# The first two attribute sets summed ahead of the main loop and placed in its last two steps

## The chip, the cores and the metric

One core of a Trainium2 chip runs the kernel. The time is device microseconds of one execution, the median of three runs: 729.02 us before (729.01 to 731.43). The engines are named as in the profile: PE (TensorE), DVE (VectorE), ACT (ScalarE), POOL (GpSimd) and SP (SyncE, which issues most of the DMAs). PEld is PE's weight load.

## The reference

A graph of 6250 nodes with 128 features and 206250 edges sorted by destination. The first layer normalizes and linearly maps the nodes, batch-normalizes them, and sums neighbours weighted by degree. The second one sums the edge attributes by destination and runs a three-layer MLP.

```python
h = jnp.maximum(_layernorm(x), 0.0)
# _L0: H = batchnorm(h @ W.T + b);  dinv = rsqrt(1 + segment_sum(ones, dst))
#      out = relu(segment_sum(H[src] * dinv[src] * dinv[dst], dst) + H * dinv**2)
x = x + _L0_gnn_ref(h, W, b, gamma, beta, src, dst)
h = jnp.maximum(_layernorm(x), 0.0)
agg = jax.ops.segment_sum(edge_attr, dst, num_segments=N)
h1 = relu(concat([h, agg, u[batch]]) @ W1 + b1)
x = x + relu(h1 @ W2 + b2) @ W3 + b3
```

## The kernel before

Data-dependent sums are made as matmuls with one-hot matrices that DVE makes by comparing indices with an iota. The program has four stages, each a block of one queue for each engine, with a barrier between blocks.

**First stage** (block at L401, to 67.7 us). The destinations are turned, the degrees counted: `make_hot` (9 batches on DVE), `count` (PE), `make_low`, `make_blocks`, `weigh_blocks` (DVE), `place_degrees` (PE). Beside it the 13 chunks of x (512 nodes; the last has 106) are normalized by DVE, ACT or POOL (`BY_POOL`, `BY_ACT`, the rest DVE; those of POOL lie in `h_far`, the others in a ring of 4), turned and mapped by PE (`turn_h`, `apply_linear`), saved by ACT, and measured by DVE (`bn_part`, L589). At the end of DVE's queue stand the span of the chunks (L615 to L619), `find_scale`, the last parts, `bn_aggr` and `begin_pass`. POOL's last work is a memset of `acc[:, 1]`, where the attribute sums are gathered later and where x lies until all chunks are normalized.

**Table stage** (block at L970, 69.9 to 114.8 us). For each chunk c: PE turns the rows (`turn_rows`, L1000) into one of three banks, ACT saves a high half (L1078), DVE a low half (`save_low_part`, L1187), PE turns both back for the self term (`turn_self`), ACT saves that. Between the chunks DVE plans where each node's edges begin, POOL gathers the sources by 17 indirect DMAs (L977), DVE splits them into low part and key (`split_sources`, 5 batches), PE turns them (`turn_keys`), ACT saves them. 16 spare tiles take what didn't fit (`key_spares` on DVE, `turn_spares` on PE, `save_spares`). At the end DVE makes the first four batches of one-hots of tiles (`hot_of_tiles`) and the attribute one-hots of set 0 (`hot_of_attr`, L904). SP loads attribute set 0 and the MLP's weights.

**Main loop** (L1396, 116.6 to 660 us). 27 steps of 80 tiles (step 17 has 16). For each tile PE builds counts (L1596), ACT evicts them by fours (L1442), and in the step after they are multiplied with the table, 98 matmuls of 240 columns (L1606). DVE makes the one-hots by eights, four batches ahead. Beside this each step handles one attribute set: 3 kinds x 5 x 4 matmuls of 128x128 f32 against 32-column one-hots (`sum_attr`, L1616; 120 records for the three kinds) into `ps_sums`, at tile 24 (`SUM_AT`; 56 from step 18 on); ACT copies them to `sums_sb` (L1451), PE places them by a one-hot from POOL (`place`, L1642) at tile 40 (72 from step 18 on), and DVE adds the windows to `acc[:, 1]` at `starts` (`add`, L1517). `summed` frees the three attribute buffers in turn: SP then loads the next set into them (1.28 MB each), and DVE makes its one-hots. PE waits for all of them (`ready_to_sum`, `ready_to_place`) in the tiles just before.

**Tail** (to 728.4 us): layer norm and MLP of the 13 chunks, with x loaded again once the last sums are made.

## Time and profile before

| | us |
|---|---|
| median of 3 runs | 729.02 (729.01 to 731.43) |
| profiled execution | 730.38 |
| its span, first to last instruction | 728.4 |
| PE busy | 666.4 (91%) |
| DVE busy | 568.1 (78%) |
| ACT busy | 456.6 (63%) |
| POOL busy | 141.8 (19%) |
| mean granted clock of PE | 0.974 |

Busy shares are a mean over stages with different limits: in the main loop PE is full, in the table stage DVE is. In the rows, an idle time before an instruction stands in brackets with what ended it; merged instructions carry their count (xN).

### The profile page before, as it was taken

The page shows a single profiled execution, that of the slowest core. Times are in us where ns is not written, and L with a number is a line of the kernel's source. Part 1 is how long each engine was busy: PE and PEld are TensorE (multiplying, and loading weights), DVE is VectorE, ACT ScalarE, POOL GpSimd, SP SyncE. Part 2 cuts the span into 40 slices and gives each one's busy share as a digit, 9 for nine tenths or more (in the row PEclk, how much of TensorE's full clock was granted, in tenths as well). Part 3 has the DMA queues.
Part 4 walks back from the last instruction along what each step waited for, and adds up shares of the span by engine and source line. Part 5 has one row for each costly group of instructions (what it writes and reads, how often), then busy time and mean ns, then how long its engine had stood idle before and what let it go on. Part 6 is the DMA issues. An engine that isn't in the chain of part 4 may idle for free. (4 is left out here: it accounts for less than half of the span.)

```text
span 728.4 us, 21542 instructions
## 1 busy us (share of the span) xinstructions
PE 666.4 (91%) x9010; PEld 572.3 (79%) x9010; DVE 568.1 (78%) x1114; ACT 456.6 (63%) x811; POOL 141.8 (19%) x184
## 2 busy tenths in 40 slices
PE   3994675899999999999999999989999999998997
PEld 2763564688888888888888888979888888896554
DVE  7888996988888888888889887588888888835632
ACT  4471682767766666666676666276666776666862
POOL 8503840111111111101111111010000000003622
PEclk9997696999999999999999999999999999999999
DMA  9000611645565554444455555465445555660122
GB/s 264 8 1 23 245 35 45 231 173 207 218 219 216 216 208 174 179 172 177 178 210 216 216 216 217 155 219 206 179 175 176 199 216 216 216 173 4 40 62 76
DMA packets 64972, 119.75 MB, mean 164 GB/s; under 512 B 3170, under 2 KB 22832, under 8 KB 64900
## 3 DMA queue, kind: packets, MB, share of 16 engines
q1 hardware_dynamic: 63332, 117.82, 46.1%
q0 software_dynamic: 576, 1.12, 0.6%
q8 instruction: 34, 0.56, 0.3%
q10 hardware_dynamic: 1008, 0.07, 0.1%
q14 instruction: 22, 0.18, 0.1%
HBM read 115.81 MB, written 4.03 MB: 165 GB/s over the span
## 5 line engine op out<-in xcount | busy, mean ns | idle before, releaser
L1606 PE MATMUL ps_product<-counts_sb,table_sb 128*128 128x240 f16 (+1 forms) x2646 | 408.5, 261 | 0.0
L1442 ACT CAST counts_sb<-ps_counts 128x588 f16<-128x588 f32 x524 | 335.8, 649 | 103.1 <-PE ps_counts L1596 59.7
L1596 PE MATMUL ps_counts<-key_hot,lo_hot 128*128 128x147 bf16 x2096 | 384.6, 231 | 16.4 <-issue 7.5
L1606 PEld LDWEIGHTS ps_product<-counts_sb,table_sb 128*128 128x128 f16 x2646 | 240.2, 97 | 8.1
L1596 PEld LDWEIGHTS ps_counts<-key_hot,lo_hot 128*128 128x128 bf16 x2096 | 198.1, 98 | 61.4 <-ACT counts_sb L1442 17.9
L898 DVE TENSOR_TENSOR key_hot<-key,iota_key 128x1176 bf16<-128x1176 f16 x262 | 199.8, 763 | 0.0
L894 DVE TENSOR_TENSOR lo_hot<-src_lo,iota_key 128x1024 bf16<-128x1024 f16 x262 | 180.8, 690 | 17.9 <-PE ps_counts L1596 15.6
L1426 POOL TENSOR_SCALAR place_hot<-iota_c,slot_now 128x96 f32<-128x96 f32 x81 | 58.7, 737 | 468.5 <-PE ps_place L1642 454.4
L904 DVE TENSOR_TENSOR attr_hot<-rel,iota_w 128x640 f32<-128x640 int16 x81 | 66.6, 824 | 57.6 <-PE ps_sums L1616 57.5
L1616 PE MATMUL ps_sums<-attr,attr_hot 128*32 128x128 f32 x3240 | 95.6, 276 | 0.0
L1616 PEld LDWEIGHTS ps_sums<-attr,attr_hot 128*32 128x32 f32 x3240 | 88.2, 111 | 4.5 <-issue 4.1
L1451 ACT COPY sums_sb<-ps_sums 128x384 f32<-128x384 f32 x27 | 12.9, 478 | 89.0 <-PE ps_sums L1616 89.0
L1517 DVE TENSOR_TENSOR acc<-acc,ps_place 128x96 f32 x81 | 20.5, 253 | 20.9 <-PE ps_place L1642 12.3
L1805 DVE TENSOR_TENSOR y_ring<-ps_three,x_ring 128x512 f32<-128x512 f32 (+1 forms) x13 | 8.6, 659 | 29.4 <-PE ps_three L1915 23.2
L977 POOL DMA_INDIRECT src_raw<-src_padded,begin_int x17 | 21.6, 1271 | 5.4 <-issue 4.9
L1642 PE MATMUL ps_place<-place_hot,sums_sb 128*128 128x96 f32 x162 | 22.0, 272 | 0.0
L873 ACT ACTIVATE attr<-attr,nodes_below 128x128 f32<-128x128 f32 x49 | 20.2, 496 | 0.8 <-DVE nodes_below L864 0.8
L1783 POOL TENSOR_TENSOR x_ring<-attr,b_rows 128x512 f32<-128x512 f32 (+1 forms) x13 | 15.6, 1204 | 25.7 <-DVE y_ring L1805 25.7
L1642 PEld LDWEIGHTS ps_place<-place_hot,sums_sb 128*128 128x128 f32 x162 | 20.2, 191 | 0.0
L1852 ACT ACTIVATE z_ring<-ps_one,cols 128x512 f32<-128x512 f32 (+1 forms) x13 | 8.7, 673 | 16.0 <-PE ps_one L1904 16.0
L1893 PE MATMUL ps_two<-z_ring,w_sb 128*128 128x512 f32 (+1 forms) x26 | 13.6, 606 | 4.7 <-ACT z_ring L1859 2.5
L1078 ACT ACTIVATE table_sb<-ps_rows,dinv 128x128 f16<-128x128 f32 x49 | 14.0, 390 | 5.6 <-PE ps_rows L1000 5.6
(294 smaller groups left out, 526.7 us busy)
## 6 DMA issues: line engine op xcount, KB each, us to landing
attr<-in_edge_attr_dram SPq DMA_DIRECT2D x80, 1280.0 KB, 8.2
acc<-in_x_dram SPq DMA_DIRECT2D x4, 768.0 KB, 9.4
attr<-in_x_dram SPq DMA_DIRECT2D x12, 256.0 KB, 5.2
out_dram<-y_ring SPq DMA_DIRECT2D x12, 256.0 KB, 2.3
src_padded<-in_src_dram SPq DMA_DIRECT2D x1, 805.5 KB
attr<-in_edge_attr_dram SPq DMA_DIRECT2D x2, 320.0 KB, 8.1
attr<-in_edge_attr_dram SPq DMA_DIRECT2D x1, 640.0 KB, 3.9
raw_d<-in_dst_dram SPq DMA_DIRECT2D x1, 480.0 KB
```

Of the source, the lines that this page charges most:

```text
L873: ins = act.activation(h2_ring[:, c % 2, k * P:(k + 1) * P], x_again[:, n, :], ACT.Relu, scale=rstd[:, n:n + 1], bias=shift[:, n:n + 1])
L894: v.tensor_tensor(lo_hot[:, held], src_lo[:, tiles].rearrange("p (b c) -> p b c", c=2).unsqueeze(2).to_broadcast(whole), iota_lo[:].unsque ...
L898: v.tensor_tensor(key_hot[:, held], key[:, tiles].rearrange("p (b c) -> p b c", c=2).unsqueeze(2).to_broadcast(whole), iota_key[:].unsquee ...
L904: v.tensor_tensor(attr_hot[:, r], rel[:, r, :, s * CG:(s + 1) * CG].unsqueeze(3).to_broadcast(whole), iota_w[:].unsqueeze(1).unsqueeze(1). ...
L977: pool.indirect_dma_start(src_raw[:, k, :], None, src_elements, bass.IndirectOffsetOnAxis(ap=begin_int[:, k:k + 1], axis=0))\
L1426: pool.tensor_scalar(place_hot[:, n % R, :], iota_c[:], slot_now[:, kind, s:s + 1], None, ALU.is_equal).then_inc(place_hots, 1)
L1442: act.copy(counts_sb[s % 2][:].rearrange("p h (n t) -> p h n t", n=WN) [:, :, :, k * QUAD:(k + 1) * QUAD], ps_counts[n % 2][:, :, 0:KEYS]. ...
L1517: v.tensor_tensor(win, win, ps_place[:, kind * WC:(kind + 1) * WC], ALU.add)\
L1596: ins = pe.matmul(ps_counts[quad % 2][:, c, 0:KEYS], lo_hot[:, held, pair, :, q % 2], key_hot[:, held, pair, :, q % 2], start=True, stop=True)
L1606: ins = pe.matmul(ps_product[side][:, 0:SLOTS] if tiles == TS else product, table_sb[:, h, low, :], counts_sb[side][:, h, :] if tiles == T ...
L1616: ins = pe.matmul(ps_sums[g * W:(g + 1) * W, j * P:(j + 1) * P], attr_hot[:, j, t, g, :], attr[:, j * CG + g, t * P:(t + 1) * P], start=(t ...
L1642: pe.matmul(ps_place[:, j * WC:(j + 1) * WC], sums_sb[:, j, :], place_hot[:, j, :], start=True, stop=True).then_inc(placed, 1)
```

## The change

Attribute sets 0 and 1 are summed by PE in the table stage: set 0 behind `turn_rows(5)`, `turn_self(3)` and `plan_before` into the bank `ps_lows`, set 1 at the very end into a bank of `ps_rows`. ACT saves them (`save_early`) to `early_sums`, which lies over `drel`, no longer needed. The one-hots of set 0 are made at the end of the first stage on DVE, those of set 1 between `split_sources(3)` and `hot_of_tiles(0)`. SP issues set 1's loads as set 0's sums are made, and set 2's loads as set 1's are. The main loop sums sets 2 to 26 in steps 0 to 24, and steps 25 and 26 only place sets 0 and 1 (`set_of_place`). Step 0 sums at tile 56 and places at 72; its attribute one-hots stand between batches 4, 5, 6 and 7.

In the first stage POOL normalizes chunks 4 and 7 too, DVE's small work (scale, span, `make_low(0)`, `make_blocks(0)`) moves between the degree one-hots, and the memset of `acc[:, 1]` is cut into a piece for each chunk, each behind the chunk's normalization, and one for the end.

```diff
+        drel_flat = sb("drel", [P, R * GB * GT], I16)
+        drel = drel_flat[:].rearrange("p (g t) -> p g t", t=GT)
...
+        EARLY = 2
+        LATER = STEPS - EARLY
+        attr_hot = sb("attr_hot", [P, R, GT, CG, W])
+        early_hots, early_summed, early_saved = (sem(n, ctx) for n in ("early_hots", "early_summed", "early_saved"))
+        early_in = [sem(f"early_in{r}", ctx) for r in range(R)]
+        early_sums = drel_flat[:, 0:2 * EARLY * R * P].bitcast(F32)\
+            .rearrange("p (e j f) -> p e j f", e=EARLY, j=R)
+
+        def set_of_place(s):
+            return s + EARLY if s < LATER else s - LATER
+
+        def hot_of_attr(engine, s, r, made):
+            whole = [P, GT, CG, W]
+            engine.tensor_tensor(attr_hot[:, r], rel[:, r, :, s * CG:(s + 1) * CG].unsqueeze(3).to_broadcast(whole),
+                                 iota_w[:].unsqueeze(1).unsqueeze(1).to_broadcast(whole), ALU.is_equal)\
+                  .then_inc(made, 1)
+
+        def early_hot(engine, e):
+            for r in range(R):
+                if e >= 1:
+                    engine.wait_ge(early_summed, (e - 1) * R + r + 1)
+                hot_of_attr(engine, e, r, early_hots)
...
-            BY_POOL, BY_ACT = (5, 8, 11), (2, 3, 6, 9)
+            BY_POOL, BY_ACT = (4, 5, 7, 8, 11), (2, 3, 6, 9)
...
-                    pool.wait_ge(h_by_pool, len(BY_POOL))
-                    pool.wait_ge(h_by_dve, len(BY_DVE))
-                    pool.wait_ge(h_by_act, len(BY_ACT))
-                    pool.memset(acc[:, 1, :], 0.0)
+                    for c in range(CHUNKS):
+                        h_is_ready(pool, c)
+                        pool.memset(acc[:, 1, c * NC:c * NC + width(c) * P], 0.0)
+                    pool.memset(acc[:, 1, NB * P:], 0.0)
...
-                    normalize(4)
-                    for b in range(4, BATCHES):
-                        make_hot(v, b)
+                    make_hot(v, 4)
+                    make_hot(v, 5)
                     make_low(v, 0)
+                    make_hot(v, 6)
+                    make_hot(v, 7)
+                    v.wait_ge(w_in, 16 * W_LOADS)
+                    find_scale(v, link)
+                    find_span()
                     link(make_blocks(v, 0))
-                    normalize(7)
+                    make_hot(v, 8)
                     bn_part(0)
                     bn_part(1)
...
                     for c in range(5, 8):
                         bn_part(c)
-                    v.tensor_copy(chunk_start[:], chunk_row[:, 0, :].rearrange("a (r s) -> a s r", r=R))
-                    link(v.tensor_tensor(chunk_row[:, 1, :], chunk_row[:, 1, :], chunk_row[:, 0, :], ALU.subtract))
-                    link(v.tensor_reduce(span_row[:, 1:2], chunk_row[:, 1, :], AX.X, ALU.max))
-                    link(v.tensor_scalar(span_row[:, 0:2], span_row[:, 0:2], 0.0, None, ALU.max))
-                    v.tensor_copy(span_int[:], span_row[:, 0:2])
-
-                    v.wait_ge(w_in, 16 * W_LOADS)
-                    find_scale(v, link)
                     for c in range(8, CHUNKS):
                         ins = bn_part(c)
                     link(ins)
                     v.bn_aggr(bn[:, 0:2], bstats[:].rearrange("p c k -> p (c k)")).then_inc(bn_ok, 1)
                     begin_pass(v, link)
+                    early_hot(v, 0)
                     v.wait_ge(placed_deg, CC)
...
+        def load_early(sp):
+            for e in range(1, EARLY):
+                for r in range(R):
+                    sp.wait_ge(early_summed, (e - 1) * R + r + 1)
+                    load_attr(sp, e * R + r, CG, early_in)
+            for r in range(R):
+                sp.wait_ge(early_summed, (EARLY - 1) * R + r + 1)
+                load_attr(sp, EARLY * R + r, CG, attr_in)
+
+        def sum_set(pe, sums, j, summed_up):
+            for t in range(GT):
+                for g in range(CG):
+                    ins = pe.matmul(sums[g * W:(g + 1) * W, j * P:(j + 1) * P], attr_hot[:, j, t, g, :],
+                                    attr[:, j * CG + g, t * P:(t + 1) * P], start=(t == 0), stop=(t == GT - 1))
+            ins.then_inc(summed_up, 1)
+
+        def sum_early(pe, e, sums):
+            for j in range(R):
+                pe.wait_ge(early_hots, e * R + j + 1)
+                pe.wait_ge(early_in[j], 16 * (e + 1))
+                sum_set(pe, sums, j, early_summed)
+
+        def save_early(act, e, sums):
+            act.wait_ge(early_summed, (e + 1) * R)
+            act.copy(early_sums[:, e].rearrange("p j f -> p (j f)"), sums[:, 0:R * P]).then_inc(early_saved, 1)
...
+                        if c == 5:
+                            sum_early(pe, 0, ps_lows)
                         if c == 7:
+                            pe.wait_ge(early_saved, 1)
                             turn_keys(0)
...
                     turn_spares(pe, spare_keys_at, spare_lows_at, spares_keyed, spares_turned)
+                    pe.wait_ge(low_ready, CHUNKS)
+                    sum_early(pe, 1, ps_rows[0][:].rearrange("p b f -> p (b f)"))
...
                         if c == 6:
+                            save_early(act, 0, ps_lows)
                             save_low(0)
...
+                    save_early(act, 1, ps_rows[0][:].rearrange("p b f -> p (b f)"))
...
                     split_sources(3)
+                    early_hot(v, 1)
                     v.wait_ge(keys_saved, 1)
                     hot_of_tiles(v, 0, 0)
                     split_sources(4)
                     key_spares(v, link, spare_in, spares_keyed)
                     for b in range(1, HELD):
                         hot_of_tiles(v, b, b * OCT)
-                    for r in range(R):
-                        hot_of_attr(v, 0, r)
                     save_spares(v, spare_keys_at, spare_lows_at, spares_turned)
...
+                    load_early(sp)
...
-                            for a in range(R, CC):
+                            for a in range((EARLY + 1) * R, CC):
                                 c, r = divmod(a, R)
-                                sp.wait_ge(summed, a - R + 1)
+                                sp.wait_ge(summed, a - (EARLY + 1) * R + 1)
...
-                                sum_at, place_at = ((LATE_SUM_AT, LATE_PLACE_AT) if s > SHORT else (SUM_AT, PLACE_AT))
+                                sum_at, place_at = ((LATE_SUM_AT, LATE_PLACE_AT) if s > SHORT or s == 0 else
+                                                    (SUM_AT, PLACE_AT))
                                 for b in range(HELD if s == 0 else 0, OCTS):
                                     make_oct(s, b)
+                                    if s == 0 and b < HELD + R:
+                                        make_attr_hot(b - HELD)
                                     if s == LATE and b == 2:
                                         make_attr_hots(s)
                                     if s == LATE and b == 3:
                                         add(SHORT)
                                     if s >= 2 and s != LATE + 1 and b == 3:
                                         take_product(s - 2)
...
-                                    if s < STEPS - 1 and b == min(sum_at // OCT + 2, OCTS - 1):
+                                    if s + 1 < LATER and b == min(sum_at // OCT + 2, OCTS - 1):
                                         make_attr_hots(s + 1)
-                                    if s < SHORT and b == place_at // OCT + 3:
+                                    if 0 < s < SHORT and b == place_at // OCT + 3:
                                         add(s)
-                                    if s > LATE and b == 1:
+                                    if (s > LATE or s == 1) and b == 1:
                                         add(s - 1)
...
+                                early = like == 8
                                 for q in range(TS):
-                                    if q == sum_at - 1:
+                                    if q == sum_at - 1 and not early:
                                         pe.wait_ge(attr_hots, s * R + R)
                                     build_tile(quads, octs, q, first, OCTS * odd)
                                     if q == LAG and like >= 3:
                                         pe.wait_ge(taken, s - 2)
-                                    ready_to_sum(s, first, sum_at - q)
-                                    ready_to_place(s, first, place_at - q)
+                                    if not early:
+                                        ready_to_sum(s, first, sum_at - q)
+                                    ready_to_place(s, first, place_at - q, early)
...
-                                        sum_attr(s)
+                                    if q == sum_at and not early:
+                                        sum_attr()
                                     if q == place_at:
-                                        place(s)
+                                        place(early_sums[:, s - LATER] if early else sums_sb)
...
-                            with pe.Fori(LATE // 2 + 2, (STEPS + 1) // 2) as i:
+                            with pe.Fori(LATE // 2 + 2, (LATER + 1) // 2) as i:
                                 step(i, 1, 7)
                                 step(i, 0, 7)
+                            step((LATER + 1) // 2, 1, 8)
+                            step((LATER + 1) // 2, 0, 8)
...
```

## Rows read from the trace of the kernel before

**Rows 1.** the page: busy shares, and TensorE's granted clock in 40 slices (tenths)

```profile
PE 666.4 (91%) x9010; PEld 572.3 (79%) x9010; DVE 568.1 (78%) x1114; ACT 456.6 (63%) x811; POOL 141.8 (19%) x184
...
PEclk9997696999999999999999999999999999999999
```

**Rows 2.** timeline (start us, us, engine line operation), TensorE, two late steps

```profile
620.63 3.48 PE L1616 MATMUL ps_sums<-attr,attr_hot 128*32 128x128 f32 x120
624.05 0.24 PE L1596 MATMUL ps_counts<-key_hot,lo_hot 128*128 128x147 bf16 x1
...
640.73 3.48 PE L1616 MATMUL ps_sums<-attr,attr_hot 128*32 128x128 f32 x120
```

**Rows 3.** windows: us, busy of the engines, granted clock, DMA share, GB/s

```profile
70.00:83.00 13.00, 9.49 (x64) 8.00 (x65) 12.19 (x46) 7.17 (x24) 9.47 (x9) 0.50 0.95 337
...
84.00:90.00 6.00, 3.33 (x35) 2.54 (x35) 5.96 (x17) 2.64 (x9) 5.09 (x4) 1.00 0.14 36
94.00:110.00 16.00, 10.49 (x166) 8.98 (x163) 14.38 (x46) 14.44 (x38) 6.27 (x8) 1.00 0.11 27
110.00:116.60 6.60, 0.00 (x0) 0.00 (x0) 4.77 (x9) 0.00 (x0) 0.39 (x1) 0.57 0.00 0
116.60:123.00 6.40, 5.67 (x61) 4.19 (x65) 2.75 (x4) 3.60 (x6) 1.15 (x3) 0.50 0.02 5
124.80:135.30 10.50, 7.96 (x117) 5.40 (x105) 9.31 (x16) 8.22 (x15) 2.70 (x3) 1.00 0.99 368
```

**Rows 4.** timeline of TensorE in step 0 and at the start of step 1

```profile
116.62 1.17 PE L1596 MATMUL ps_counts<-key_hot,lo_hot 128*128 128x147 bf16 x8 [7.48 <-issue]
118.04 1.23 PE L1596 MATMUL ps_counts<-key_hot,lo_hot 128*128 128x147 bf16 x8 [0.25 <-ACT counts_sb L1442]
...
121.17 5.10 PE L1616 MATMUL ps_sums<-attr,attr_hot 128*32 128x128 f32 x120
126.19 0.66 PE L1596 MATMUL ps_counts<-key_hot,lo_hot 128*128 128x147 bf16 x7
...
131.76 1.00 PE L1596 MATMUL ps_counts<-key_hot,lo_hot 128*128 128x147 bf16 x8 [0.19 <-ACT counts_sb L1442]
...
135.98 0.26 PE L1606 MATMUL ps_product<-counts_sb,table_sb 128*128 128x240 f16 x1
...
140.03 2.17 PE L1616 MATMUL ps_sums<-attr,attr_hot 128*32 128x128 f32 x72
```

**Rows 5.** timeline of the first stage's end, POOL, DVE and ACT

```profile
57.19 5.39 POOL L503 MEMSET acc<- 128x6346 f32 x1 [24.81 <-DVE h_ring L571]
...
59.46 3.15 DVE L618 TENSOR_SCALAR span_row<-span_row 1x2 f32<-1x2 f32 x1
...
61.09 0.35 ACT L682 ACTIVATE acc<-turn,cols 128x106 f32<-128x106 f32 x1 [2.03 <-PE turn L755]
...
64.06 2.64 DVE L589 BATCH_NORM_STATS2 bstats<-acc 128x6 f32<-128x512 f32 x5
...
67.54 0.19 DVE L629 TENSOR_TENSOR dinv<-dinv,ps_x 128x49 f32<-128x49 f32 x1
```

**Rows 6.** timeline of the first stage's middle, POOL and DVE

```profile
25.64 6.74 POOL L497 TENSOR_SCALAR h_far<-acc,rstd,shift 128x128 f32<-128x128 f32 x12 [4.15 <-DVE shift L129]
...
36.34 1.35 DVE L274 TENSOR_TENSOR deg_hot<-drel,iota_deg 128x1080 bf16<-128x1080 int16 x2 [2.34 <-PE ps_y L309]
```

**Rows 7.** timeline of the table stage about chunk 6, PE and DVE

```profile
85.52 0.66 PE L1000 MATMUL ps_rows<-ident,acc 128*128 128x128 f32 x4
...
90.18 1.12 DVE L1187 SCALAR_TENSOR_TENSOR table_sb<-ps_rows,dinv,table_sb 128x128 f16<-128x128 f32 x4
```

**Rows 8.** timeline of the table stage's start and end, SP, PE and DVE

```profile
69.95 2.64 SPq L880 DMA_DIRECT2D attr<-in_edge_attr_dram  x3
...
108.93 0.21 PE L242 MATMUL ps_plan<-ident,spare_lows 16*128 16x16 f32 x1
...
112.33 2.28 DVE L904 TENSOR_TENSOR attr_hot<-rel,iota_w 128x640 f32<-128x640 int16 x3
```

More of the change, by code:

```diff
@@ L1330, in gnn_kernel, with _ @@
                     with nc.Block() as block:
+                        @block.sync
+                        def _(sp):
+                            for a in range(R):
+                                load_attr(sp, a, CG, early_in)
+                            load_early(sp)
+                        @block.scalar
+                        def _(act):
+                            for e in range(EARLY):
+                                save_early(act, e, ps_sums)
                         @block.gpsimd
@@ L1355, in _ @@
                             first_hots_of_pass(v)
+                            for e in range(EARLY):
+                                early_hot(v, e)
                 with nc.Fori(0, chunk_passes) as chunk_pass:
@@ L1636, in ready_to_place, with place @@
                                     pe.wait_ge(added, s * R)
[L1637 removed]
+                                if before == 1 and not early:
                                     pe.wait_ge(sums_saved, s + 1)
[L1640 removed]
+                            def place(sums):
                                 for j in range(R):
[L1642 removed]
+                                    pe.matmul(ps_place[:, j * WC:(j + 1) * WC], sums[:, j, :], place_hot[:, j, :],
                                               start=True, stop=True).then_inc(placed, 1)
```

80 lines of the change are left out of this document (35 added, 45 removed).

## The prediction

> **What bounds the kernel now.** I read the page first [rows 1]: TensorE (PE) is busy for 91% of the span, and its clock digits have one weak stretch, slices 4 to 7. Next comes the spacing of like events in the main loop. Two neighbouring blocks of attribute sums start at 620.63 and 640.73, so a late step takes 20.10 us, and the first build behind the block starts at 624.05 [rows 2]: a block of 120 matmul records holds PE for 3.42 us. PE has work without a pause there and sets the pace, so what leaves its queue is time.
>
> Then the windows by stage [rows 3]. From 70 to 83 the granted clock stood at 0.50, which is 1.2 of its 2.4 GHz; in 84 to 90 and 94 to 110 it was 1.00. In this table stage (69.9 to 114.8) PE is far from full and VectorE (DVE) nearly is: 14.38 of 16 us in 94 to 110. So added DVE or queue time costs there, added PE time not always. In step 0 the block of sums took 5.02 us (121.17 to 126.19) [rows 4], because the clock was still 0.50 from 116.6 to 123 [rows 3].
>
> The first stage ends on DVE. Its 1x2 tensor_scalar (L618) lasted from 59.46 to 62.61, and the memset on GpSimd (POOL) ended at 57.19 + 5.39 = 62.58; only then came the scale and the last five bn parts (64.06 to 66.70), and DVE ended at 67.73 [rows 5]. ScalarE (ACT) had saved the last linear chunk by 61.44, having waited 2.03 us for PE [rows 5]: PE sets that time.
>
> **Steps 25 and 26.** They now hold no sums; step 25 places set 0 and step 26 set 1. PE keeps 80 builds, 98 multiplies and the place. What could be late next is the eviction or DVE. But between two blocks the loop already runs 20.10 - 3.42 = 16.68 us at a stretch without sums, ACT and DVE keeping up. So this is 2 x 3.42 = **-6.8 us**. The extra unrolled PE code I cost at nothing: steps 0 to 2 and 18 to 20 are unrolled already.
>
> **Step 0.** Its sums (now set 2) move from tile 24 to 56, its place from 40 to 72. Before, tile 0 starts at 116.62 and the first product, behind the fifth tile of step 1, at 135.98 [rows 4]; less 0.6 for those builds, the step took 18.7. The block now falls after the clock has risen: 5.02 becomes 3.42, -1.6. Eight builds come every 1.42 us at the low level (116.62 to 118.04) and every 1.00 + 0.19 = 1.19 at the full one [rows 4]; two more eights now lie ahead of the rise, 2 x 0.23 = +0.4. Estimate **-1.2**, step 0 being 17.5. DVE has three attr hots between its first batches; at 2.28/3 = 0.76 each [rows 8] the batch for tile 56 is ready just in time.
>
> **Wait for set 3.** Its three loads are issued as set 2's sums end. Before, the same three transfers moved from 124.8 to 135.3 (10.5 us at 0.99 of the DMA engines) [rows 3], to 9.1 behind the end of the sums at 126.2 [rows 4]. Now the sums end near T0 + 12.9 (T0 is tile 0), so the data are there at T0 + 22.0 to 22.6. Step 1 wants them at tile 23: its block came 4.05 behind the first product (140.03), so about 4.5 behind its tile 0, T0 + 22.0. Estimate **+0.4**, bounds 0 and 1.0. Later sets have a whole step of 20 us.
>
> **First stage.** POOL normalizes two more chunks, 8 more instructions at 6.74/12 = 0.56: it ends near 36.9 instead of 32.4 [rows 6], each chunk before PE wants it. DVE loses chunks 4 and 7. It idled 2.34 us for PE's counting before hot 6 [rows 6], and once more as long before hot 8; make_low(0), scale and span (1.45 us behind L618 and some 0.7 ahead of it [rows 5]) now fill this. The memset goes in fourteen pieces, 0.43 us for 512 of 6346 columns, the last ones near 56. DVE then has bn parts 5 to 11 done and waits for 61.44. Behind it come the last part (106 columns, about 0.3 by 2.64/5 = 0.53 for a full one), then the aggregate, begin_pass and dinv, 66.70 to 67.73 = 1.03 [rows 5]. New there is early_hot(0), three attr hots: 2.28 [rows 8]. End: 61.44 + 0.1 + 0.3 + 1.03 + 2.28 = 65.1, against 67.73: **-2.6**. Bounds: -2.8, and 0 if DVE loses its slack of some 2 us before 61.
>
> The L618 row shows a DVE instruction that ended with the POOL memset beside it. The Trainium skill, "SBUF — State Buffer", section "Who interferes with whom", says that a tensor_scalar in a two-port mode and a GpSimd instruction lock each other out for the whole instruction. That speaks against the new order, since pieces of the memset now meet the scale's and span's four tensor_scalars: by it up to 4 x 0.43 = 1.7 us, which the slack holds; were it all on the path, the sum would be 1.7 less good.
>
> **Table stage, set 0.** SP issues the three loads first, as it did [rows 8]; they fill the DMA engines until about 84 (0.95 in 70 to 83, 0.14 in 84 to 90) [rows 3]. PE takes the block ahead of turn_rows(6), which started at 85.52 [rows 7]. The clock was 1.00 there, so 3.42 us: the rows of chunk 6 are turned at 89.5, and ACT, which needs about as long for them as DVE (1.12), has them at 90.8. DVE began low part 6 at 90.18 [rows 7]: 0.6 late. ACT then holds save_early, one copy, ahead of save_low(0), and PE's turn_keys(0) waits for both; DVE has other work meanwhile. Estimate +0.3, bounds 0 and +3.4 (the block at half the clock).
>
> **Table stage, set 1.** early_hot(1) costs DVE 2.28 and the old attr hots are gone: 0. But the hots stand ahead of split 4 and key_spares, so turn_spares, over at 109.1 [rows 8], now ends near 111.3. Only behind it comes the second block, with PE idle for some 2.3 us before: 114.7 at the full level, 118.1 at half of it. The clock did fall back after 109.1 (mean 0.57 in 110 to 116.6) [rows 3]. Step 0's block of 5.02 is 56 records at half rate (3.2 us) and 64 at full; I take the same mix again here, 5.0, ending 116.3 less 0.1 to 0.3 of lead: 116.1. Behind it SP must still issue the last of set 2's loads, 2.64/3 = 0.88 [rows 8], with ACT's copy beside it: 117.0. Before, DVE's hots ended at 114.61 [rows 8] and two small copies at 114.8. **+2.2**, bounds +0.7 and +4.1. Set 2 lands near 126, 9.1 behind these sums' end by the same pattern as set 3, and step 0 wants it at about 128.
>
> Set 1's own load runs from 87 to 99 beside the gathers of src. Splits 2 to 4, which need the later gathers, stand behind low part 12 in DVE's order, so I cost this at nothing; bound +1.
>
> **Sum.** -6.8 - 1.2 + 0.4 - 2.6 + 0.3 + 2.2 = **-7.7 us**. The profiled execution took 730.38 us for a span of 728.4; it would be 722.7. The median of the runs is 729.02, and 729.0 - 7.7 = **721.3**.
>
> **The rivals.** (A) *All fits.* The second block runs at the full level (+0.7), the first costs nothing, set 3 is in time: -9.9, **719.1**. For it: the clock was 1.00 through 94 to 110 with PE idle a third of that time; against it: the longer idle stretch. (B) *The early sums are paid for.* One of the two blocks runs wholly at half the clock, or DVE waits for gathers behind set 1's load: -7.7 + 3.1 = -4.6, **724.4**, and with both 726.3. For it: 13 us at 0.50 at the stage's start, and a DVE without slack; against: 1.00 from 84 on. (C) *The first stage gives nothing.* DVE comes later than 61.4 by more than it gains, or PE does: -7.7 + 2.6 = -5.1, **723.9**. For it: PE works without a pause up to there, so a late h chunk moves the end. (D) *Slower than before.* The blocking wait for set 0 sits in the middle of PE's queue, with rows, tables and keys of all later chunks behind it; each microsecond that the third load lands past 86 goes through ACT to DVE. It eats the gain of 7.7 from about 94 on; if the loads take twice their 14 us (to 98), the stage is 12 longer: **733**. Against it: the DMA engines were free from 84 to 90 (0.14) [rows 3]. (E) That the sums don't leave the loop is excluded: PE's queue of steps 25 and 26 holds none.
>
> **How the numbers follow.** Forecast 721.3 (720.0 to 722.6) 0.45; A 0.18; B 0.17; C 0.13; D 0.02; between or beyond these 0.05. The range takes in A and B's first price, with the half microsecond on either side that the small terms leave open: 718.4 to 724.9. B's upper part, D and the tails are left out. A measurement here tells about 0.5% (3.6 us): faster than 725.4 has 0.92, within it 0.06, slower 0.02.
>
> **What would show it.** In the changed profile: the first stage's last DVE instruction at about 65.1, and the span's tensor_scalar short; a block of 3.4 us near 83 (2.6 earlier than 85.5) and one of 3.4 to 6.8 at the end of the table stage; PE's first build within 0.5 of 116.6; step 0's block at 3.42; at most 1 us of PE idle before step 1's; no block in the loop's last two steps, whose places lie 16.7 us apart. The forecast is wrong if these steps take 20 us, if DVE waits in the table stage for more than 3 us in all, or if PE's clock falls inside the loop.

## The result, and the profile after

The changed kernel took **735.2 us** (median of 6 runs, 732.0 to 736.0) against 729.1 (728.7 to 731.5) for the kernel before on the same chip: ratio 1.0058, 95% interval 1.0035 to 1.0082 (taken over all runs, so it is not that of the two medians). It is slower by some 0.6%, where 721.3 with a range of 718.4 to 724.9 was forecast. Its profiled execution took 736.01 us for a span of 734.1. The executions of each kernel spread by some microseconds (see the first stage below), so most of what follows compares stretches of the profiled executions.

The stretches, each from its two end marks in the two traces:

| stretch | before | after | difference | forecast |
|---|---|---|---|---|
| start to DVE's last operation of the first stage | 67.73 | 67.00 | -0.73 | -2.6 |
| from there to the last operation of any engine in the table stage | 47.04 | 49.60 | +2.56 | +2.5 |
| from there to PE's first build in the main loop | 1.85 | 7.95 | **+6.10** | 0 |
| first build to ACT's copy of step 1's sums | 26.96 | 31.39 | **+4.43** | -0.8 |
| the steps behind it, to the copy of step 24's sums | 460.52 | 460.60 | +0.08 | 0 |
| from there to the end | 124.30 | 117.56 | -6.74 | -6.8 |
| sum | 728.4 | 734.1 | +5.7 | -7.7 |

The page of the changed kernel (busy shares, granted clock in 40 slices, and the main loop's multiplies with what ended the idle time before them), beside [rows 1]:

```profile
PE 672.2 (92%) x9010; PEld 577.4 (79%) x9010; DVE 565.3 (77%) x1106; ACT 457.3 (62%) x811; POOL 150.4 (20%) x205
...
PEclk9997686799999999999999999999999999999999
...
L1677 PE MATMUL ps_product<-counts_sb,table_sb 128*128 128x240 f16 (+1 forms) x2646 | 408.8, 261 | 2.8 <-DMA attr<-in_edge_attr_dram 2.8
```

The loop now has a stall on a load of attributes that it didn't have. The timeline shows the rest of it. The end of the table stage and the entry into the main block, PE first, then ACT, POOL and SP:

```profile
112.37 0.26 PE L240 MATMUL ps_plan<-ident,spare_lows 16*128 16x16 f32 x1
112.56 3.48 PE L921 MATMUL ps_rows<-attr,attr_hot 128*32 128x128 f32 x120
...
124.55 1.17 PE L1667 MATMUL ps_counts<-key_hot,lo_hot 128*128 128x147 bf16 x8 [8.50 <-issue]
...
116.12 0.48 ACT L933 COPY drel<-ps_rows 128x384 f32<-128x384 f32 x1 [3.44 <-PE ps_rows L921]
...
118.06 1.55 POOL L1494 TENSOR_SCALAR place_hot<-iota_c,slot_now 128x96 f32<-128x96 f32 x3 [16.05 <-issue]
...
113.93 2.55 SPq L905 DMA_DIRECT2D attr<-in_edge_attr_dram  x3
```

Set 1's block runs at the full rate (3.48 us), and the last operation of the stage ends at 116.12 + 0.48 = 116.60, with SP's last issue over at 116.48. POOL is in the main block at 118.06. PE is there 6.49 us later, waiting for nothing that the profile names ("issue"). In the kernel before, POOL's first operation of the block started at 116.21 and PE's first build at 116.62 [rows 4], 0.41 apart:

```profile
116.21 1.54 POOL L1426 TENSOR_SCALAR place_hot<-iota_c,slot_now 128x96 f32<-128x96 f32 x3 [14.11 <-issue]
```

What PE did in this time stands in the view by source line, which lists branches too. It is the jump over the block that this data never enters, `If(slot_pass > 0)`, on PE's sequencer (PEldq). The line is executed twice, at 117.7 and 668.5 after the change; its shortest, median and longest time are in ns, after and then before:

```profile
L1423 PEldq COMPARE_BRANCH  x2: 82/3192/6302, 117.7 to 668.5; - x2
```
```profile
L1356 PEldq COMPARE_BRANCH  x2: 82/158/234, 115.9 to 663.1; - x2
```

The first of the two took 6.30 us in place of 0.23. The same branch took 0.07 us at most on every other engine.

Then step 0 and the start of step 1 on PE, which answer to [rows 4], and the window of the builds (columns as in [rows 3]):

```profile
130.21 1.23 PE L1667 MATMUL ps_counts<-key_hot,lo_hot 128*128 128x147 bf16 x8 [0.19 <-ACT counts_sb L1510]
131.63 1.23 PE L1667 MATMUL ps_counts<-key_hot,lo_hot 128*128 128x147 bf16 x8 [0.19 <-ACT counts_sb L1510]
133.04 1.23 PE L1667 MATMUL ps_counts<-key_hot,lo_hot 128*128 128x147 bf16 x8 [0.18 <-ACT counts_sb L1510]
...
134.76 4.31 PE L921 MATMUL ps_sums<-attr,attr_hot 128*32 128x128 f32 x120
139.00 0.66 PE L1667 MATMUL ps_counts<-key_hot,lo_hot 128*128 128x147 bf16 x7
...
150.67 0.38 PE L1677 MATMUL ps_product<-counts_sb,table_sb 128*128 128x240 f16 x1 [2.82 <-DMA attr<-in_edge_attr_dram]
...
151.30 4.56 PE L921 MATMUL ps_sums<-attr,attr_hot 128*32 128x128 f32 x120
```
```profile
124.55:136.00 11.45, 9.99 (x81) 6.66 (x85) 10.00 (x15) 8.43 (x14) 0.00 (x0) 0.50 0.12 46
```

All eights of step 0 run at the low level, 1.42 us apart, until the block of sums starts. In step 1 PE stands still for set 3's loads, and the block behind that stall takes 4.56 us.

### The profile page after: what moved, and what is told of

It is laid out like the page before. It is cut to its first block and busy times, and to the rows that moved or that the text cites. A ratio compares the mean times of both kernels' runs of the same rounds, so it can differ in the third digit from the quotient of the medians.

```text
span 734.1 us, 21496 instructions
## 1 busy us (share of the span) xinstructions
PE 672.2 (92%) x9010; PEld 577.4 (79%) x9010; DVE 565.3 (77%) x1106; ACT 457.3 (62%) x811; POOL 150.4 (20%) x205
## 3 DMA queue, kind: packets, MB, share of 16 engines
HBM read 115.81 MB, written 4.03 MB: 163 GB/s over the span
## 5 line engine op out<-in xcount | busy, mean ns | idle before, releaser
L1667 PEld LDWEIGHTS ps_counts<-key_hot,lo_hot 128*128 128x128 bf16 x2096 | 199.2, 98 | 61.9 <-ACT counts_sb L1510 17.8
L921 PE MATMUL ps_sums<-attr,attr_hot 128*32 128x128 f32 x3000 | 89.0, 277 | 0.0
L921 PEld LDWEIGHTS ps_sums<-attr,attr_hot 128*32 128x32 f32 x3000 | 82.0, 112 | 4.4 <-issue 3.9
L1707 PE MATMUL ps_place<-place_hot,sums_sb 128*128 128x96 f32 x150 | 20.4, 272 | 0.0
L1707 PEld LDWEIGHTS ps_place<-place_hot,sums_sb 128*128 128x128 f32 x150 | 18.7, 191 | 0.0
```

Of the source, the lines that this page charges most:

```text
L921: ins = pe.matmul(sums[g * W:(g + 1) * W, j * P:(j + 1) * P], attr_hot[:, j, t, g, :], attr[:, j * CG + g, t * P:(t + 1) * P], start=(t == ...
L1667: ins = pe.matmul(ps_counts[quad % 2][:, c, 0:KEYS], lo_hot[:, held, pair, :, q % 2], key_hot[:, held, pair, :, q % 2], start=True, stop=True)
L1707: pe.matmul(ps_place[:, j * WC:(j + 1) * WC], sums[:, j, :], place_hot[:, j, :], start=True, stop=True).then_inc(placed, 1)
```

## Experiments

Eleven more kernels ran; e11 is the changed kernel once more. "Entry gap" is the time from POOL's first operation in the main block to PE's first build there; "step 0/1" is the time from that build to the copy of step 1's sums.

| kernel | code PE jumps over, added | set 2's loads meanwhile | entry gap | step 0/1 | ratio to before (95%) |
|---|---|---|---|---|---|
| before | 0 | none | 0.41 | 26.96 | 1 |
| changed | 120 matmuls | yes | 6.49 | 31.39 | 1.0058 (1.0035-1.0082) |
| e11, changed again | 120 | yes | 6.54 | 31.99 | 1.0075 (1.0046-1.0105) |
| e1 | 120 | a quarter | 3.97 | 31.86 | 1.0063 (1.0047-1.0080) |
| e2, from before | 0 | 3.8 MB, other | 0.40 | 26.98 | 0.9998 (0.9981-1.0015) |
| e3 | 120 | none | 3.63 | 34.65 | 1.0072 (1.0045-1.0099) |
| e4 | 120 | yes | 6.61 | 30.21 | 1.0120 (1.0097-1.0143) |
| e5 | 0 | yes | 0.40 | 31.47 | 0.9989 (0.9968-1.0010) |
| e6, from before | 120 | none | 4.03 | 26.89 | 1.0062 (1.0037-1.0086) |
| e7 | 120 | yes | 6.43 | 27.25 | 0.9984 (0.9956-1.0012) |
| e8 | 60 | yes | 0.62 | 32.39 | 0.9987 (0.9964-1.0009) |
| e9 | 60 | yes | 0.63 | 29.12 | 0.9937 (0.9906-0.9967) |
| e10 | 120 | yes | 6.54 | 27.79 | 0.9992 (0.9966-1.0018) |

**The gap ahead of the first build.** In the first four kernels, Theory 1 was that PE's next instructions come behind set 2's loads, and Theory 2 that the larger program of PE makes the change of block slow whatever the loads do.

e1 makes set 2's loads a quarter as large:

```
-                load_attr(sp, EARLY * R + r, CG, attr_in)
+                load_attr(sp, EARLY * R + r, 1, attr_in)
```

> The changed kernel, with set 2's three loads at the end of the table stage cut to a quarter (one group of four; the other three groups keep set 1's rows, so set 2's sums are not the reference's). Theory 1 (PE's next instructions come over the DMA engines and stand behind these loads): the traffic after the stage ends 7.5 us sooner, and the gap from the last instruction of the table stage (116.6) to PE's first build falls from 7.9 us to 2 to 4; the time falls by 4 to 6 us. Theory 2 (the longer PE program makes the block change slow, whatever the DMAs do): the gap stays at 7.9 and the time moves by less than 1 us. The wait for set 3 in step 1 stays at about 3 us in both.

Measured: 734.3 us (732.3 to 734.8), gap 3.97. The loads are worth 2.5 us of the gap, and 4 us stay (0.4 of them as in the kernel before).

e2 gives the kernel before the same traffic, from DRAM to DRAM, at the same place:

```
+                    sp.wait_ge(spares_turned, 1)
+                    for a in range(R):
+                        sp.dma_start(spill[a], edge_attr[...]...).then_inc(spilled, 16)
```

> The kernel before, with three DMAs of 1.28 MB each from DRAM to DRAM, issued by SP once PE has turned the spares (109.1), that nobody reads. Nothing else is changed. Theory 1: they keep the DMA engines busy until 10 to 20 us later, and PE's first build, now at 116.6, comes 4 to 12 us later; the time rises by as much. Theory 2: PE starts at 116.6 to 117, and the time is within 1 us of the kernel before, since no load is wanted before 122.

Measured: 729.5 (728.0 to 733.2), gap 0.40. Traffic alone does nothing: Theory 1, as it stood, is refuted.

e3 issues set 2's loads only behind PE's first build:

```
+                            sp.wait_ge(built, 1)
+                            for r in range(R):
+                                load_attr(sp, EARLY * R + r, CG, attr_in)
```

> The changed kernel, with set 2's loads moved from the end of the table stage into the main loop's queue of SP, behind PE's first quad of builds. Theory 1: the gap before the first build falls from 7.9 us to about 1.9, the sums of step 0 then wait for set 2 (landing some 12 us behind the start, wanted at 10): 2 us of it go back, so 3 to 4.5 us less in all than the changed kernel. Theory 2: the gap stays, and the wait comes on top: 2 us more than the changed kernel.

Measured: 735.3 (732.1 to 737.5), gap 3.63, and PE then waited for set 2 in step 0. So 3.2 us of the 6.1 that were added have nothing to do with the loads. Two rivals were left. Theory 3: the cost lies in code that PE jumps over. In the `If(slot_pass > 0)` block, which this data never enters, the change had put the early sums as 120 unrolled matmuls. Theory 4: PE always takes some 7 us from its last matmul of the table stage to its first build (109.14 to 116.62 before), and is now last in the stage.

e5 takes those never-executed matmuls out of the changed kernel:

```
-                            for e in range(EARLY):
-                                if e >= 1:
-                                    pe.wait_ge(early_saved, e)
-                                sum_early(pe, e, ps_sums)
```

> The changed kernel without the 120 matmuls of the early sums in the block for later slot passes, which this data never enters: every instruction that is executed stays as it was, PE's program is only shorter just ahead of the main block. Changed kernel: 735.2 us; PE's first build at 124.55, 6.5 us behind POOL's entry into the block. Theory 3 (code that PE jumps over has to be fetched past): the first build comes 0.4 to 1 us behind POOL's entry, that is at about 118.5 to 119.5, and the time is 729 to 731. Theory 4 (PE's own path from the last instruction of the table stage to the first build takes some 7 us whatever it jumps over, and it is now last in the stage): first build and time unchanged, 124 to 125 and 735.

e6 puts as many into the same block of the kernel before:

```
+                            for e in range(2):
+                                for j in range(R):
+                                    for t in range(GT):
+                                        for g in range(CG):
+                                            pe.matmul(ps_sums[...], attr_hot[:, j, t, g, :], attr[...], ...)
```

> The kernel before with 120 more matmuls in the block for later slot passes, which this data never enters: nothing that is executed is changed, PE's program is longer just ahead of the main block. Kernel before: 729.1 us; PE's first build at 116.62, 0.4 us behind POOL's entry. Theory 3 (code that PE jumps over has to be fetched past): first build some 3 us later, at 119.5 to 120, time about 732. Theory 4 (PE's own path from its last instruction of the table stage counts): PE ends that stage at 109 as before, so first build at 116.6 and time 729.

Measured: e5 729.7 (725.6 to 731.2) with a gap of 0.40, e6 734.3 (733.1 to 738.1) with a gap of 4.03. PE's and POOL's lines at the entry, of e5 and then of e6:

```profile
119.00 1.54 POOL L1490 TENSOR_SCALAR place_hot<-iota_c,slot_now 128x96 f32<-128x96 f32 x3 [17.23 <-issue]
...
112.03 4.96 PE L921 MATMUL ps_rows<-attr,attr_hot 128*32 128x128 f32 x120
119.40 0.72 PE L1663 MATMUL ps_counts<-key_hot,lo_hot 128*128 128x147 bf16 x8 [2.41 <-issue]
```
```profile
119.93 1.54 POOL L1434 TENSOR_SCALAR place_hot<-iota_c,slot_now 128x96 f32<-128x96 f32 x3 [14.45 <-issue]
...
112.66 0.21 PE L242 MATMUL ps_plan<-ident,spare_lows 16*128 16x16 f32 x1
...
123.96 1.17 PE L1604 MATMUL ps_counts<-key_hot,lo_hot 128*128 128x147 bf16 x8 [11.10 <-issue]
```

e5 executes what the changed kernel executes, and e6 what the kernel before executes. In e5 PE goes from its last sum (116.99) to its first build in 2.41 us, so Theory 4 is refuted too. Theory 3 is shown from both sides: 120 matmuls that are never run cost 3.2 (e3) to 3.6 us (e6), and 6.1 with set 2's loads in flight.

The branch itself shows it in all thirteen traces. Here it is in e6 and in e8 (60 matmuls, see below):

```profile
L1364 PEldq COMPARE_BRANCH  x2: 82/1957/3832, 119.6 to 670.3; - x2
```
```profile
L1425 PEldq COMPARE_BRANCH  x2: 82/264/447, 115.5 to 661.3; - x2
```

It takes 0.23 us in before, e2 and e5, 0.44 to 0.45 in e8 and e9, 3.44 to 3.83 in e3, e1 and e6, and 6.24 to 6.42 in the five with 120 matmuls and the full loads. The DMA records say more. In each of the eight traces with 120 matmuls, one packet of the kind "instruction" (16 KB, on queue 8) moves while the branch lasts, and the branch ends 1.31 to 1.42 us behind it. It starts 1.0 to 1.25 us into the branch in e3, e6 and e1, and 3.57 to 3.65 us into it where set 2's loads fill the queues. In the other five traces no such packet moves during the branch. So PE waits there for code to be fetched, and loads in flight put off the fetch, which is what Theory 1 had right. One link is inferred: the records don't say for which engine a packet is.

**Step 0.** e7 puts its sums back to tile 24, its place back to tile 40, and DVE's three one-hots together ahead of it (DVE's lines left out here):

```
-                                sum_at, place_at = (LATE_SUM_AT, LATE_PLACE_AT) if like >= 5 or first else (SUM_AT, PLACE_AT)
+                                sum_at, place_at = (LATE_SUM_AT, LATE_PLACE_AT) if like >= 5 else (SUM_AT, PLACE_AT)
```

> The changed kernel with step 0 put back: its sums at tile 24 and its products at tile 40, as in the kernel before, and DVE makes the three one-hots of set 2's attributes at once in step 0. From the first build to the copy of step 1's sums the changed kernel takes 31.39 us, the kernel before 26.96. Theory: the difference is the clock, which the 60 dense matmuls of the sums block at tile 24 raised and the builds alone do not, and the wait for set 3's loads, which leaves with it, as they are issued 8 us sooner. Then the stretch is 27.0 and the time 735.2 - 4.4 = 730.8. Rival (the wait moves on: set 3's loads or the one-hots made at the step's start hold PE up): the stretch stays over 29 and the time over 733.

Measured: 729.4 (725.6 to 732.4); step 0/1 took 27.25 us in place of 31.39. The sums at tile 56, meant as a gain of 1.2 us by the prediction, cost 4.1 with the wait for set 3 that comes of them.

e10 keeps tile 56 and makes set 3's loads a quarter as large; e11 is the changed kernel beside it:

```
-                                load_attr(sp, a, groups, attr_in)
+                                load_attr(sp, a, 1 if a < (EARLY + 2) * R else groups, attr_in)
```

> The changed kernel with the three loads of set 3, issued as step 0's sums end, a quarter as large; three quarters of set 3's rows keep what set 2 left there. From PE's first build to the copy of step 1's sums the changed kernel took 31.39 us, the kernel before 26.96, and PE waited 2.82 us for set 3 in it. If the wait is the larger cause: the stretch is 31.39 - 2.82 = 28.6 and the time 2.8 us below the changed kernel's; the 1.6 us that stay over the kernel before are the clock. If the wait only hides another one (the one-hots of set 3, PE's own pace), the stretch stays at 30 or more. The gap ahead of the first build stays at 6 to 8 us behind PE's last sum in both.

> The changed kernel itself, on the same chip and in the same rounds as e10_quarter_set3, for the comparison of the two and for a second look at it. Theory 3 and the load's wait: as in its first profile, PE's first build 6 us or more behind POOL's entry, 31.4 us from there to the copy of step 1's sums, and 735. If the gap ahead of the first build was an accident of the first profile, the first build comes within 1 us of POOL's entry.

Measured: e10 731.2 (727.6 to 733.0), e11 736.9 (733.2 to 738.9), before 731.1 beside them. PE at step 1 in e10, then in e11:

```profile
148.12 3.48 PE L921 MATMUL ps_sums<-attr,attr_hot 128*32 128x128 f32 x120
```
```profile
152.09 0.32 PE L1677 MATMUL ps_product<-counts_sb,table_sb 128*128 128x240 f16 x1 [2.68 <-DMA attr<-in_edge_attr_dram]
...
152.65 4.90 PE L921 MATMUL ps_sums<-attr,attr_hot 128*32 128x128 f32 x120
```

Without the wait the stretch is 27.79, against 31.99 in e11: 4.2 us less, of which 2.7 are the wait and 1.4 the block behind it (4.90 against 3.48). That leaves 0.8 us over the kernel before for step 0's low clock and late block. The expectation had put the wait at 2.8 and the clock at 1.6; the stall has its own cost in clock behind it. The medians differ by 5.8 us, the two profiled executions by 6.1; in these, 1.6 of the 1.9 us beyond this stretch lie in the first stage, which ended at 65.89 in e10 and at 67.49 in e11.

**The first stage.** e4 gives the changed kernel the old order of the first stage, with the new one-hots of set 0 kept at its end:

```
-                    make_hot(v, 4)
-                    make_hot(v, 5)
+                    normalize(4)
+                    for b in range(4, BATCHES):
+                        make_hot(v, b)
...
-                        pool.memset(acc[:, 1, c * NC:c * NC + width(c) * P], 0.0)
+                    pool.memset(acc[:, 1, :], 0.0)
```

> The changed kernel with the first stage of before (chunks 4 and 7 on DVE, one memset, span and scale at the end), early_hot(0) kept at its end. If the reordering of the first stage gained what its forecast says, this is 4.9 us slower than the changed kernel (67.7 + 2.3 against 65.1 where it should have ended). By the trace of the changed kernel, where that stage ended at 67.0, it is 3.0 us slower: 70.0 to 67.0. If the new order itself made PE late there (its matmuls ran at half rate until about 40.4 instead of 36.2), PE ends at 61.0 again here and the time is 1 us slower or less.

Measured: 737.2 (735.6 to 739.0). That is 2.0 us above the changed kernel by the medians and 0.6% by the ratios (1.0120 against 1.0058), so the times alone can't tell an expectation of 4.9 from one of 3.0; the traces can. The start of PE's last row of matmuls in the stage (two of `turn`) against DVE's end, over all traces: in the old order 60.62 and 67.73 (before), 64.02 and 71.13 (e2), 64.34 and 71.43 (e6), that is 7.1 us every time, and in e4, with the 2.28 us of one-hots more, 58.62 and 67.94, that is 9.3. In the new order, one-hots included, nine traces give 4.34 to 4.36, from 58.11 and 62.46 (e9) to 63.29 and 67.63 (e3). The gain is 2.76 us, as far as the new order doesn't move PE's own end. That end lies anywhere from 58.1 to 64.3, in either order; the means are 61.9 and 62.1, from which a shift of a microsecond can't be excluded. What moves it is PE's rate: its counting matmuls start 0.100 us apart at first and 0.055 apart from 31 us in e4, 35.8 in before, some 41 in the changed kernel and 43 in e6, and the last row then starts at 58.62, 60.62, 62.65 and 64.34. (In e1, e3, e5 and e11 the rate rises at 36 to 37, but the granted clock is 0.50 again from 53 to 57.) Both orders have early and late ones. Between before and e2, which run the same work, this is all of the difference of the spans (3.4 of 3.4 us); between the two profiles of the changed kernel it is 0.5 of 2.1.

**Both repairs.** e8 is e7 with the 120 matmuls as a loop over the two sets, 60 in the program, for all data:

```
-                            for e in range(EARLY):
-                                if e >= 1:
-                                    pe.wait_ge(early_saved, e)
-                                sum_early(pe, e, ps_sums)
+                            with pe.Fori(0, EARLY) as e:
+                                for j in range(R):
+                                    pe.wait_ge(early_hots, e * R + j + 1)
+                                    pe.wait_ge(early_in[j], e * 16 + 16)
+                                    sum_set(pe, ps_sums, j, early_summed)
+                                pe.wait_ge(early_saved, e + 1)
```

> Step 0 put back as in e7_step0_at_24, and in the block for later slot passes the early sums as a loop over the two sets, 60 matmuls of code in place of 120; it computes what the changed kernel computes on any data. e5 (no such code) had PE's first build 0.40 us behind POOL's entry and 729.7, e7 (step 0 put back, 120 matmuls) 6.4 us and 729.4. If the two causes are separate, their gains add: with 60 matmuls jumped over for free the first build is 0.4 us behind POOL's entry and the time 729.4 - 5.5 = 723.9. If any code beyond what the kernel before had costs in proportion, the gap is about 3 us and the time about 726.5. If the causes overlap (the same late start counted twice), the time stays at 728 to 729.5.

Measured: 730.2 (725.2 to 731.5), no better than e5 or e7 alone. The gap is gone (0.62), but PE is now early enough to meet set 2's loads in step 0:

```profile
122.38 0.30 PE L1668 MATMUL ps_counts<-key_hot,lo_hot 128*128 128x147 bf16 x1 [2.21 <-DMA attr<-in_edge_attr_dram]
125.62 0.30 PE L1668 MATMUL ps_counts<-key_hot,lo_hot 128*128 128x147 bf16 x1 [2.94 <-DMA attr<-in_edge_attr_dram]
125.86 5.70 PE L921 MATMUL ps_sums<-attr,attr_hot 128*32 128x128 f32 x120
```

The gap of 6.5 us had hidden these loads in e7. With it gone, a wait of 2.21 + 2.94 = 5.15 us and a block of 5.70 us, mostly at the low level, took its place.

e9 takes set 1 off the end of the table stage, so that set 2's loads start sooner:

```
                     for b in range(2, KEY_BATCHES):
                         turn_keys(b)
+                        if b == 2:
+                            pe.wait_ge(low_ready, CHUNKS)
+                            sum_early(pe, 1, ps_rows[0][:].rearrange("p b f -> p (b f)"))
...
-                    split_sources(3)
                     early_hot(v, 1)
+                    split_sources(3)
```

> e8_looped_pass_code with the sum of set 1 taken off the end of the table stage: DVE makes its one-hots ahead of the split of the fourth batch of sources, PE sums it between the third and fourth batch of keys, ScalarE copies it ahead of the last two batches of keys. In the changed kernel PE's block ran 112.5 to 116.0 with its copy to 116.6, behind DVE's last operation at 115.9. Expected: block at 107.5 to 111, set 2's loads issued by 112, PE and ScalarE done before DVE, POOL's entry at 117.2 in place of 118.0 to 119.0, and the time 1 to 2 us below e8. Rival: the block delays the keys that are behind it on PE, and with them DVE's end; then DVE ends after 117 and the time is that of e8 or more.

```profile
102.75 3.48 PE L921 MATMUL ps_rows<-attr,attr_hot 128*32 128x128 f32 x120
...
112.56 1.17 PE L1669 MATMUL ps_counts<-key_hot,lo_hot 128*128 128x147 bf16 x8 [4.61 <-issue]
...
118.27 0.31 PE L1669 MATMUL ps_counts<-key_hot,lo_hot 128*128 128x147 bf16 x1 [1.65 <-DMA attr<-in_edge_attr_dram]
```

Measured: **726.4** (721.7 to 729.5, 8 runs), ratio 0.9937 (0.9906 to 0.9967): faster than the kernel before and than the changed one. That is a gain of 0.6%, and by the medians 3.9 us below e8, where 1 to 2 were expected. Set 1's block is over at 106.2, and the wait in step 0 falls from 5.15 to 1.65 us. DVE ends the stage 45.8 us after it starts, as in e8 (45.9), so the rival, keys that come late to DVE, is refuted. From DVE's last operation of the first stage to the last of the table stage it is 48.0 us in place of 48.7. This profiled execution (721.7) is the fastest of its runs, with PE early in the first stage; the median is the fair number.

## Why the prediction was wrong, step by step

**Steps 25 and 26** (-6.8): right, -6.74. The last two places lie 16.56 us apart (636.15 and 652.71), without sums.

**"The extra unrolled PE code I cost at nothing"**: this step failed, and it is the larger error. I looked only at code that is executed in the loop, and took the 1.85 us between the stage's end and the first build as fixed. 120 matmuls in a block that is skipped make it 7.95 (+6.10), and PE's branch over that block takes 6.30 us in place of 0.23. None of the five rivals had it. e5 and e6 show it; e8 and e9 show that 60 cost 0.2 us. Nothing in the trace of before shows this price. A bound from both sides was owed there, as for any resource that the trace doesn't show, and not a zero.

**Step 0** (-1.2, forecast 17.5): wrong in sign. First build to first product of step 1 was 19.45 us (124.55 to 144.00), less 0.6: 18.85, and +0.1 in place of -1.2. I had the clock rise behind the third eight, as in [rows 4], where the block of sums at tile 24 stood just there. Without that block the eights stayed 1.42 us apart through all seven, at 0.50 in the window of 124.55 to 136, and the block took 4.24 in place of 3.42. PE did nothing but builds in this time, and the granted clock rose only as the block of sums ran; before, that block had stood 32 tiles earlier. In all thirteen traces the rise lies inside step 0's block, at tile 24 as at tile 56.

**Wait for set 3** (+0.4, bounds 0 and 1.0): mis-sized, 2.8 of stall and 1.1 to 1.4 on the block behind it. I read "the data are there" from a window that ends at 135.3, 9.1 us behind the sums. The windows of after show what that leaves out, and the trace of before had it too (second block):

```profile
148.00:149.00 1.00, 0.00 (x0) 0.00 (x0) 1.00 (x2) 0.54 (x1) 0.00 (x0) 1.00 0.69 261
149.00:150.00 1.00, 0.00 (x0) 0.00 (x0) 0.17 (x1) 0.00 (x0) 0.00 (x0) 1.00 0.10 38
150.00:151.00 1.00, 0.33 (x3) 0.28 (x3) 0.00 (x0) 0.00 (x0) 0.00 (x0) 0.58 0.01 3
```
```profile
135.30:136.00 0.70, 0.56 (x6) 0.36 (x7) 0.70 (x2) 0.70 (x2) 0.00 (x0) 1.00 0.17 63
136.00:137.00 1.00, 1.00 (x13) 0.93 (x13) 1.00 (x3) 0.79 (x2) 0.00 (x0) 1.00 0.05 18
```

Most of set 3 is there by about 149, but the last packets follow one another at a tenth of the DMA engines. The last of them ends at 150.19, and PE goes on at 150.67, 11.6 behind the end of the sums (139.07). In the kernel before, the loads were complete at 137.24, 11.0 behind the sums: this, and not 9.1, was the term to take. With the sums ending only at T0 + 14.5 in place of 12.9, the two errors add. With 0.1 for step 0, 2.8 for the stall, 1.1 for the block behind it and 0.4 between the products beside the stall, they make +4.43 where -0.8 stood.

**First stage** (-2.6): the mechanism and the size were right, -2.76. The 65.1 was reckoned from a last matmul at 60.62; in this execution PE started it at 62.65, and DVE 4.35 later, at 67.00. The rest is the scatter of PE's rate in this stage, which I didn't know to be there from one profile. POOL's chunks took longer than forecast, 20 instructions in 13.94 us, and ended at 39.86 in place of 36.9; PE didn't wait for them. The span's tensor_scalar was to be short, and that sign didn't come: it waited longer than the 1.7 us forecast at most. The slack held this too, as DVE's end stayed 4.34 to 4.36 behind PE's in all nine traces. It met the pieces of the memset, here in the changed kernel and in e5:

```profile
40.38 0.23 DVE L611 TENSOR_REDUCE span_row<-chunk_row 1x1 f32<-1x81 f32 x1
40.63 2.04 DVE L612 TENSOR_SCALAR span_row<-span_row 1x2 f32<-1x2 f32 x1
...
39.80 4.45 POOL L523 MEMSET acc<- 128x512 f32 x9
```
```profile
40.45 3.53 DVE L612 TENSOR_SCALAR span_row<-span_row 1x2 f32<-1x2 f32 x1
...
39.72 4.25 POOL L523 MEMSET acc<- 128x512 f32 x9
```

By the Trainium skill, "SBUF — State Buffer", section "Who interferes with whom", a tensor_scalar in a two-port mode and a GpSimd instruction lock each other out for the whole instruction. The traces agree that it waits, but not for one piece: the pieces start some 0.47 us apart and last 0.53 each, so each starts before the one ahead of it is over. In the changed kernel the tensor_scalar ended with the sixth (42.66), behind which the row of pieces had its first gap, of 0.11 us; in e5 and e11, where it took 3.53 and 3.84 us, with the ninth and last of the row (43.97 and 43.91). Short pieces in a row did not let DVE in between.

**Table stage** (+0.3 and +2.2): the sum of 2.5 was right (2.56), but by luck, as its terms were not. Set 0's block ran at half rate, and DVE waited for it:

```profile
85.25 5.16 PE L921 MATMUL ps_lows<-attr,attr_hot 128*32 128x128 f32 x120
...
92.20 1.13 DVE L1237 SCALAR_TENSOR_TENSOR table_sb<-ps_rows,dinv,table_sb 128x128 f16<-128x128 f32 x4 [2.64 <-ACT table_sb L1126]
```

Low part 6 came 22.99 us after the stage's start, against 20.26 before: 2.7 late, inside the bound of 3.4 but not the 0.6 that I took. The window of 84 to 90 had 0.61 where [rows 3] had 1.00, so taking over a clock from the trace of before, in a queue that the change alters, was the weak step. Set 1's block then ran at the full level, 3.48 us and not 5.0, and gave part of it back.

**Rivals.** B's mechanism came true in part (set 0 at half rate) and D's did not: set 0 never waited for its loads. The first stage's end, only 0.73 us earlier, looks like C's, but came of the scatter. Signs of being wrong were there: DVE waited 3.5 us in the table stage (3.2 of them for ACT), PE's clock fell inside the loop (0.50 from 150.2 to 153.6), and PE's first build came at 124.55 and not near 116.6. The forecast of "faster" with 0.92 fell to a mechanism that wasn't among them.

## What to carry to other kernels

Code that is never executed is not free where an engine jumps over it with nothing to hide the jump: keep rare paths rolled up in loops, and compare the entry of each block on each engine, not only what runs in it. When work moves, ask what it did beside its own job where it stood: here TensorE's clock rose with the block of sums, which also released the next loads, and both went with it. Repairs are tested together too: two that each gave over 5 us gave no more in one kernel, since one stall had hidden the next.

## What the runs showed of the hardware

- Skipping 120 more matmuls made PE 3.2 to 3.6 us late at the next block with no loads in flight (e3 3.63, e6 4.03 against 0.40) and 6.0 to 6.2 late with 3.8 MB of loads in flight (five traces, 6.43 to 6.61). Skipping 60 cost 0.2 (e8 0.62, e9 0.63). The time lies in PE's branch: 0.23 us, 0.45 with 60, 3.4 to 3.8 and 6.2 to 6.4 with 120. In the eight traces with 120, and in no other, a packet of 16 KB of the kind "instruction" moves during it, and the branch ends 1.3 to 1.4 us behind the packet. That it is PE's own code fits this; the records don't name the engine.
- The loads start that packet late: 3.6 us into the branch with them, 1.0 without. The same traffic without the longer program (e2), or the same loads with the short one (e5), cost the entry nothing (0.40 in both).
- Three loads of 1.28 MB move at 0.99 of the DMA engines for most of their time and end in a tail of small packets: 1.2 us at 0.09 in the changed kernel. PE goes on 0.5 us after the last packet (150.19 and 150.67; 151.61 and 152.09 in e11), and then at the low level of its clock: the block behind a stall of 2.7 to 2.8 us took 4.56 and 4.90 us in place of 3.48.
- A tensor_scalar on two elements waited out a whole row of memset pieces on GpSimd, 2.0, 3.5 and 3.8 us, though each piece lasted 0.53.
